# Three small steps (16, 16 and 32 rows) in front of fifteen of 64, with the next step's rows fetched between a step's tiles

## The reference

```python
e = stack([tbl_f[ids[:, f]] for f in range(32)], axis=1)    # b, m=32, d=16
x0 = xk = e
for W in (W0, W1, W2):                                        # (32, 32 or 64, 64)
    xk = relu(einsum('bmd,bhd,mhk->bkd', x0, xk, W))
    outs.append(sum(xk, axis=2))
z = concatenate(outs, axis=1)                                 # b, 192
h = concatenate([z, dense_ctx], axis=1)
h = maximum(h @ W_top1 + b_top1, 0)                           # 512
h = maximum(h @ W_top2 + b_top2, 0)                           # 256
return h @ W_top3
```

## Time and profile before

| what | us |
|---|---|
| median of 3 runs | 625.06 |
| the profiled execution | 622.48 |
| its span, first to last instruction | 620.7 |
| PE, DVE, POOL, ACT busy | 563.6, 546.5, 488.3, 308.2 |

### The profile page before, as it was taken

How to read it: one execution, slowest core, us unless ns; L and a number is a source line. 1 busy time by engine, 2 the same in 40 slices (tenths; PEclk the granted TensorE clock), 3 DMA queues, 4 the chain that set the end, 5 groups by cost and what they waited for, 6 DMA issues and landing times.

```text
span 620.7 us, 7817 instructions
## 1 busy us (share of the span) xinstructions
PE 563.6 (91%) x2548; PEld 194.8 (31%) x2548; DVE 546.5 (88%) x321; ACT 308.2 (50%) x1345; POOL 488.3 (79%) x364
## 2 busy tenths in 40 slices
PE   0058997999999999999999999999999999999997
PEld 0012232332322333333333333333333333334354
DVE  0038997999999999999999999999999999999580
ACT  0023735355464745455476736454565736454442
POOL 6765888887889798988888788988888797949360
PEclk9997999999999999999999999999999999999998
DMA  3198878778586868788686858787776858687000
GB/s 99 29 375 315 309 249 310 274 267 295 191 314 210 316 218 311 270 299 295 223 289 215 310 199 313 261 310 274 251 275 213 289 212 311 255 306 271 2 1 0
DMA packets 52852, 150.89 MB, mean 243 GB/s; under 512 B 9830, under 2 KB 17386, under 8 KB 52810
## 3 DMA queue, kind: packets, MB, share of 16 engines
q1 hardware_dynamic: 44608, 148.27, 65.6%
q0 software_dynamic: 8192, 2.11, 2.5%
q10 hardware_dynamic: 10, 0.00, 0.0%
HBM read 147.20 MB, written 3.15 MB: 242 GB/s over the span
## 4 chain that ended last, share of the span: by engine, by line
DVE 33%; PE 29%; DMA 19%; issue 8%; POOL 8%; SPq 2%; ACT 1%; DVEq 0%; POOLq 0%
DVE prod L336 31%; PE y_ps L518 26%; DMA x0bc<-x_rows 14%; POOL emb L291 6%; DMA emb<-table,row_sb 2%; DVE z L364 2%; DMA x_rows<-emb 2%; PE x0g_ps L579 2%; POOL pool_prod L306 2%; SPq L263 1%; PE x0g_ps L584 1%; PE x0g_ps L602 0%; SPq L236 0%; SPq L246 0%; DMA off_sb<-id_offset 0%
## 5 line engine op out<-in xcount | busy, mean ns | idle before, releaser
L336 DVE TENSOR_TENSOR prod<-x0bc,x_ps 128x2048 f32<-128x2048 f32 (+1 forms) x252 | 456.5, 1887 | 13.6 <-ACT x_ps L418 13.1
L518 PE MATMUL y_ps<-prod,w_sb 128*64 128x512 f32 x1640 | 381.2, 598 | 12.2 <-DVE prod L336 12.0
L291 POOL DMA_INDIRECT emb<-table,row_sb x256 | 244.9, 957 | 65.5 <-issue 62.8
L306 POOL TENSOR_TENSOR pool_prod<-x0bc,x_sb 128x1024 f32<-128x1024 f32 x102 | 242.4, 2384 | 48.1 <-ACT x_sb L435 35.0
L518 PEld LDWEIGHTS y_ps<-prod,w_sb 128*64 128x64 f32 x1640 | 115.5, 137 | 253.4 <-issue 214.0
L425 ACT ACTIVATE relu<-y_ps 128x16 f32<-128x16 f32 x480 | 79.6, 296 | 115.3 <-PE y_ps L518 115.3
L418 ACT ACTIVATE x_ps<-y_ps 64x512 f32<-64x512 f32 x128 | 73.0, 570 | 75.4 <-PE y_ps L518 72.8
L518 PE MATMUL y_ps<-pool_prod,w_sb 128*64 128x512 f32 x408 | 104.9, 594 | 2.1 <-POOL pool_prod L306 2.0
L336 DVE TENSOR_TENSOR prod<-x0bc,x0g_ps 128x2048 f32<-128x2048 f32 x32 | 72.8, 2288 | 37.5 <-DMA x0bc<-x_rows 32.4
L435 ACT ACTIVATE x_sb<-relu 64x512 f32<-64x512 f32 x128 | 80.4, 628 | 3.4
L425 ACT ACTIVATION_READ_ACCUMULATOR relu<-y_ps 128x1 f32 x480 | 79.7, 322 | 0.0
(11 more groups left out here) (34 smaller groups left out, 71.0 us busy)
## 6 DMA issues: line engine op xcount, KB each, us to landing
x0bc<-x_rows SPq DMA_DIRECT2D x256, 512.0 KB, 7.0
x0g<-x_rows SPq DMA_DIRECT2D x16, 512.0 KB, 4.7
emb<-table,row_sb POOLq DMA_INDIRECT x256
x_rows<-emb SPq DMA_DIRECT2D x16, 128.0 KB, 2.1
w_sb<-w SPq DMA_DIRECT2D x2, 512.0 KB, 4.7
x_rows<-emb SPq DMA_DIRECT2D x16, 64.0 KB, 2.0
wt_sb<-wt SPq DMA_DIRECT2D x1, 512.0 KB
wt1a_sb<-wt_a SPq DMA_DIRECT2D x1, 256.0 KB
```

The costliest lines, as they stand in the source:

```text
L291: pool.indirect_dma_start(emb[:, turn, DIM * n:DIM * (n + 1)], None, table, bass.IndirectOffsetOnAxis(row_sb[:, at:at + 1], 0)).then_inc(g ...
L306: pool.tensor_tensor(pool_prod[:, n % POOL_RING, 0:width(s)], x0bc[:, slot(s, j), 0:width(s)], x[:, 0:width(s)], ALU.mult).then_inc(pool_p ...
L336: made = dve.tensor_tensor(out, left, right, ALU.mult)
L518: made = pe.matmul(ps[MAPS * h:MAPS * (h + 1), 0:half(s)], w, moving[:, half(s) * h:half(s) * (h + 1)], start=first, stop=final)
```

## The change

The first 64 rows become three steps of 16, 16 and 32 rows, so that there are 18 steps. Step s + 2 of before is step s + 4 now.

- The three small steps have no tiles on POOL: DVE multiplies all 16, in 8 groups a layer. ACT makes no `x_sb` copies for them.
- POOL issues the gathers of steps 0 to 4 (4, 4, 8, 16 and 16) in a row in front of its first product. From step 3 on it gathers step s + 2 between the products of step s.
- `AHEAD`: in steps 0 to 3 SP stores the next step's rows and loads its `x0g` between this step's tiles: behind 8 and 12 tiles (in step 1 behind 6 and 8). In all other steps it does so behind tile 15, which is where it was.
- The semaphores of the tiles, `bc_in`, exist twice, for even and odd steps.
- The top network's weights are loaded behind step 3's tiles (before: step 1's). The chunks hold the same rows; the first is now 6 steps of three widths, and its copies into the network's input are cut by width, 18 instead of 6.

```diff
-ROWS_OF = [64] * 16
+ROWS_OF = [16, 16, 32] + [64] * 15
-POOL_OF = {STEPS - 2: (5, 4), STEPS - 1: (5, 4)}
+POOL_OF = {0: (0, 0), 1: (0, 0), 2: (0, 0), STEPS - 2: (5, 4), STEPS - 1: (5, 4)}
+GATHERED_FIRST = 5
+AHEAD = {0: (8, 12), 1: (6, 8), 2: (8, 12), 3: (8, 12)}
-CHUNKS = [(0, 4), (4, 8), (8, 12), (12, 15), (15, 16)]
+CHUNKS = [(0, 6), (6, 10), (10, 14), (14, 17), (17, 18)]
+def copies_after(s, l):
+    return 4 * sum(1 for i in range(s + 1) if pool_tiles(i, l + 1))
...
             def load_x0g(s):
+                sp.wait_ge(scratch_out[s % 2], 32 * (s // 2 + 1))
                 if s > 0:
...
             def load_tiles(s):
-                for j in range(TILES):
+                store_at, load_at = AHEAD.get(s, (TILES, TILES))
+                for j in range(TILES + 1):
+                    if s + 1 < STEPS:
+                        if j == store_at:
+                            store_rows(s + 1)
+                        if j == load_at:
+                            load_x0g(s + 1)
+                    if j == TILES:
+                        break
                     k = TILES * s + j
                     if k >= SLOTS:
                         wait_free(k - SLOTS)
...
+            store_rows(0)
+            load_x0g(0)
             for s in range(STEPS):
-                store_rows(s)
-                sp.wait_ge(scratch_out[s % 2], 32 * (s // 2 + 1))
-                load_x0g(s)
                 load_tiles(s)
-                if s == 1:
+                if s == 3:
...
-                    if s + 2 < STEPS:
+                    if GATHERED_FIRST <= s + 2 < STEPS:
                         gather(s + 2, done, done + gathers[k])
...
             pool.wait_ge(rows_done, 2)
-            gather(1, 0, GATHERS_OF[1])
+            for s in range(1, GATHERED_FIRST):
+                gather(s, 0, GATHERS_OF[s])
...
-                if x is not None:
+                if x is not None and pool_tiles(s, l + 1):
                     act.wait_ge(relu_done[l], s + 1)
```

More of the change, by code:

```diff
@@ L205, in cin_tower_kernel @@
         x0g_in = sem("x0g_in")
-        bc_in = [sem(f"bc_in{g}") for g in range(TILES // GROUP)]
+        bc_in = [[sem(f"bc_in{i}_{g}") for g in range(TILES // GROUP)] for i in range(2)]
         w0_ready = sem("w0_ready")
@@ L262, in load_tiles @@
                         [FIELDS, QUART, width(s)])
-                    sp.dma_start(x0bc[:, slot(s, j), 0:width(s)], rows).then_inc(bc_in[j // GROUP], 16)
+                    sp.dma_start(x0bc[:, slot(s, j), 0:width(s)], rows).then_inc(bc_in[s % 2][j // GROUP], 16)
             sp.dma_start(ids_sb[:], ids).then_inc(ids_in, 16)
@@ L299, in layer @@
                 done = 0 if l == 1 else sum(GATHERS_AFTER[1])
-                pool.wait_ge(copied[l - 1], 4 * (s + 1))
+                pool.wait_ge(copied[l - 1], copies_after(s, l - 1))
                 for k, j in enumerate(pool_tiles(s, l)):
-                    pool.wait_ge(bc_in[j // GROUP], 32 * (s + 1))
+                    pool.wait_ge(bc_in[s % 2][j // GROUP], 32 * (s // 2 + 1))
                     n = pool_before((s, l)) + k
@@ L342, in layer0 @@
                 for g, group in enumerate(groups_of(s, 0)):
-                    dve.wait_ge(bc_in[g], 32 * (s + 1))
+                    dve.wait_ge(bc_in[s % 2][g], 32 * (s // 2 + 1))
                     product(s, before((s, 0)) + g, group, x0g_ps)
```

## The result

The changed kernel takes 621.98 us (median of 5 runs, 620.70 to 622.68), the one before 625.06 in the same job (5 runs). The ratio is 0.9959, 95% interval 0.9942 to 0.9977: 1.4 to 3.6 us faster, not 10. The forecast of 615.2 and its range of 611.5 to 621.5 both missed, the range by 0.5 us.

The account below looks back on a forecast made before the run. DVE paces the steady steps at 34.4 us; the gain lies in the start, where POOL's chain sets (5,0): 135.50 - 125.4 = 10.1 us, taken as 9.9, so 625.06 becomes 615.2. Range 611.5 to 621.5, 8 in 10.

Parts of the forecast that it names:

- First product 17.2: Start, step 0: tile pair landed at 17.2 us, so DVE's first product comes 18.8 us earlier.
- SP 0.65 a tile: Start, SP's queue: issuing one tile in step 0 costs SP 0.65 us.
- the 48th gather at 63.2: POOL's row of gathers in front of its first product ends with the 48th, at 63.2 us.
- Rival 4: Small steps' tiles: 1 KB packets cost as 4 KB ones, 1.3 us a tile; 628 us; chance 0.03.
- POOL's first product: Step 3, tile 13 queued behind the 48th gather's landing, step 4's store and seven transfers: 79.4 us (77 to 81).
- the chain through the gathers: From POOL's first product through the next gathers to (5,0): 46.0 us, so (5,0) not before 125.4; chance 0.48.
- DVE's own chain: DVE through the small steps, (3,1) at 74 to 78, then 48.8 us: (5,0) at 122.8 to 126.8.
- the first rival: DVE's chain decides, hand-overs adding up: (3,1) at 78 to 82, (5,0) at 127 to 131, 616.5 to 620.5; chance 0.22.
- Stores that hold up tiles: Stores of steps 1 to 3 are held up, each delaying tiles behind it some 2 us: 621; chance 0.06.
- the third rival: PE stays at half clock in the 16-row steps: (3,1) at 92, 5.3 us slower, 630 us; chance 0.07.
- The same work in the same order: Behind (5,0): same work as before from (3,0) at 135.50, 13 steps left, steps no longer than 34.4 us.
- The sum: Whole kernel: 135.50 - 125.4 = 10.1 us won at (5,0), taken as 9.9; median from 625.06 to 615.2.

Follow-up runs that it names:

- e3: Changed kernel with step 3's prefetch removed, so step 4's store and `x0g` stand behind tile 15 again: 623.11 us, ratio 0.9974.
- e1: Changed kernel with six steps of gathers in a row instead of five: 622.27 us, ratio 0.9937.
- e4: Changed kernel with the edits of e1, e2 and e3 together: 623.69 us, ratio 0.9981.
- e6: Changed kernel with six steps gathered in a row and the network's weights issued behind step 4's last tile: 622.25 us, ratio 0.9971.
- e17: Changed kernel with small steps' tiles packed side by side and step 4's rows stored behind step 3's tiles, chip without the hold: 619.72 us, ratio 0.9921.
- e7: Changed kernel with `AHEAD` empty, so every step's store and `x0g` stand behind tile 15: 628.92 us, ratio 1.0069.
- e12: The kernel before once more, unchanged, for a second trace: 623.34 us.
- the packed one: Changed kernel with small steps' tiles packed side by side and step 4's rows stored behind step 3's tiles; ratio 0.9921 in e17.
- e2: Changed kernel with the network's weights loaded behind step 5's tiles instead of step 3's: 624.93 us, ratio 1.0013.
- e13: The changed kernel again, unchanged, on a chip with the hold: 664.46 us, ratio 1.0606 against the kernel before.

## Why the prediction was wrong

- **First product 17.2, SP 0.65 a tile, the 48th gather at 63.2**: right (17.37; 5.14 us for 8 tiles; 63.11). The 128-column matmuls cost 0.074 us each (64 in 4.75 from 32.69 on), less than my 0.09, and 0.09 was itself below what my rows give, 0.16 - 0.05 = 0.11. Rival 4 (1 KB packets as dear as 4 KB) is out.
- **The failed step: POOL's first product, 67.5 + 1.2 + 0.8 + 7 x 1.34 + 0.5 = 79.4; it was 85.55.** The front part came 1.25 us late (the first of the seven issues at 70.75 instead of 69.5), all of it in the gather's landing, at 68.77 and not 67.5. My 0.8 fits what the places took, but I had named nothing for it, so that is luck. The larger part is the seven transfers: 85.4 - 70.75 = 14.65 us, 2.09 each, where I had 1.34. I priced them as a stream in full queues, but the queues had been emptied, by the wait for the gather in after and by the one for places in e3: 182 GB/s for 4 us, then 324. Over the 14.65 us the rate is 312 GB/s, at which the 3.67 MB of the seven take 11.8 us. So about 2.4 of the missing 5.3 us are the lower rate, and the other 2.9 went to bytes beside the seven, by this sum those issued behind them. P to (5,0) took 46.5 us against 46.0. That is no proof of the chain through the gathers, since it is 45.3, 45.2 and 45.3 in e1, e4 and e6 too, where that chain is cut.
- **DVE's own chain, 122.8: also wrong, by about as much.** (3,1) was at 78.89 instead of 74, since tiles landed later than the 2 to 2.5 us I gave them: 4.82 in front of (2,0), 8.99 in front of (3,0). The half clock in (1,2) adds 0.9. Behind it DVE waited 1.93 + 0.35 us at (4,0). 78.89 + 48.8 + 2.3 = 130.0 without any wait for POOL. That is the first rival, 127 to 131 and up to 622, to which I gave 0.22; e1, with the other chain cut, has (5,0) at 131.2. In e17 POOL is 3.9 us earlier and (5,0) 0.5 us, though its (3,1) is later as well. Both chains hang on the same thing, how long a tile lies in a full queue, and I counted them as independent.
- **Stores that hold up tiles**: only the last (step 4's) did. Without the moves (e7) it is 7 us worse, so the change does what it says.
- **Half clock**: it came after 35 us, which I had named as a sign of the third rival (0.50 from 45 to 51, PE idle for 2.94 us in front of its matmul at 46.55, and from 90 to 92). It cost 0.9 us and at most 0.5 more, not 15. (0,1), which I had thought might run at half clock, ran at 1.00 from 20 to 30 despite its waits for tiles.
- **"The same work in the same order" behind (5,0)**: from (5,0) to the last layer's first product it takes 458.2 us, against 455.8 and 456.5 (e12) in two traces of before from (3,0). In the kernels with small steps it is 456.9 to 459.6 where the weights don't stand in front of step 6's tiles. Some 2 us are lost there on average (458.3 against 456.2). The waits of DVE at the heads of the steps (1.62 and 1.00 the largest in after) make up most of it, but a spread of 1 us is in the traces of one kernel too; the cause is open.
- **The sum**: in the two profiled runs 3.5 us are won at (5,0), 2.4 lost from there to the last layer's first product and 0.6 behind it (30.0 us against 29.4), which leaves the 0.5 by which the spans differ. The medians are 3.1 apart, since before's profiled run lay 2.6 under its median; where in the program the usual run of before loses these is not shown. The range's upper end missed by 0.5 us because the tail of DVE's chain, up to 622, was cut off at 621.5.

On chips without the hold no version was shown to beat the changed kernel: the intervals of the packed one's 0.9921 and e1's 0.9937 overlap with that of 0.9959. On the two chips with it the packed kernel beats the changed one by 5.5 and 5.9 us, and both lose to the kernel before.

## What to carry to other kernels

Work out the start of a pipeline as several chains to the point from which all is regular, and give each transfer the time that the bytes in front of it in the queue take, not its own; a stop of the issuing engine long enough to empty the queues is paid again on restart. When two chains end within a few microseconds of each other, a fix of one gives little: seven us at the first product, different orders of gathers, weights and stores, and freer buffers all ended at (5,0) = 130 to 134 (without the moves inside the steps, e7, it is 138.4). Time a change to the start on more than one chip.

## What the runs showed of the hardware

- Landing, from issue: 2.7 us for tiles of 128 KB (median of 32), 4.2 for 256 KB, 11.5 for 512 KB between 60 and 100, though 512 KB at 390 to 410 GB/s are 1.3: the rest is queue.
- With all engines' share near 1, the rate was 388 to 412 GB/s in a long stream (e17, 65 to 81.6), 324, 320 and 322 from 74 to 80, just after the queues had been empty (after, e1, e3), and 280 to 313 where the network's weights, 1 MB in narrow rows, were in flight beside the tiles (after, 86 to 92). Their 1 MB cost about 3 us in e2 and e4.
- Two chips held each of the kernels with 16-row steps that ran there for 32 to 41 us, in three pieces, in the last of which DMA was idle (e13, 0 GB/s from 66 to 74); the chips of the other jobs never did.
- The granted clock fell from 1.00 to 0.50 (1.2 GHz) while PE was idle in front of (2,0), and cost the 16-row layer (1,2) 0.9 us of 5.75.
